# Pooled attention's denominators: from ones matmuls to running sums on ScalarE

## The chip, the cores and the metric

The kernel runs on one core of one Trainium2 chip. The metric is the device time of one execution in microseconds; the lower the better. Engines are named as in the profile: PE is TensorE, DVE VectorE, ACT ScalarE, POOL GpSimd, SP SyncE.

## The reference, cut to what matters

Four images of 256 channels and 32 x 32 pixels go through two residual blocks. The first is attention on the group-normalised image: half of it within windows of 2 x 2 pixels, half of it *pooled*, that is every pixel's query against 256 pooled windows. The second is a 3 x 3 convolution of the normalised, masked and rectified image.

```python
q = (xh.reshape(B, H * W, C) @ l_q_w).reshape(B, H * W, L_HEADS, HEAD_DIM)       # 4 heads of 32
pooled = xh.reshape(B, hg, WS, wg, WS, C).mean(axis=(2, 4)).reshape(B, G, C)     # G = 256
kv = (pooled @ l_kv_w).reshape(B, G, 2, L_HEADS, HEAD_DIM)
k, v = (kv[:, :, 0], kv[:, :, 1])
attn = jax.nn.softmax(jnp.einsum('bnhd,bmhd->bhnm', q, k) * SCALE, axis=-1)
lo = jnp.einsum('bhnm,bmhd->bnhd', attn, v).reshape(B, H * W, L_DIM)
lofi = (lo @ l_proj_w + l_proj_b).reshape(B, H, W, L_DIM)
...
x = x + _L0_conv_ref(_gn(x), ...)
x = x + _L1_conv_ref(_gn(x), ...)          # mask, relu, 3 x 3 convolution, bias
```

## The kernel before

Channels or tokens lie on the 128 partitions, and an image's 1024 pixels along the free dimension. Every engine has one program, written out by hand; semaphores tie them together, and each engine works in the order of its program. All four images go through the same steps. For TensorE an image has a *front* (projections of queries, keys and values; the scores of pooled attention; the scores of window attention) and a *rest* (exponentials' use: the value matmuls of both attentions and their output projections). The convolution of image b-1 is cut into single matmuls, and the program puts so many of them between the other steps as the tuples `FRONT` and `REST` (for image 1 `FRONT_1` and `REST_1`) say: `conv.more(fill[i])`. Half of the 144 matmuls of a convolution run in the rest of an image, the other half in the next front. In the front of image 2 another 8 (`POOL_WAIT`) go ahead of the pooled keys, in that of image 3 they go behind `fill[12]`. There are four PSUM tiles of two banks: `slot[0..2]` and `cps`, in which the convolution alternates between two banks. A new position of the convolution (`V_SUM`, `V_DIFF`, `V_LEFT`, `V_RIGHT`) begins only when VectorE has added the result of the position before the last to the image (`conv_result`).

Pooled attention needs the scores twice. In the front, TensorE makes eight blocks of *local scores* (L1113, tokens on partitions, 4 heads x 256 keys), which go round over three PSUM slots (`LA_SLOT`). VectorE takes the row maxima of each block (`maxima`, L848). A block may use its slot when the maximum three blocks ahead of it is done. The 32 columns of maxima are turned by TensorE (L1351), split into two parts (`maxima_parts`) and sent by SP's DMA into two more rows of the queries, so that the second scores (`pooled_scores`, keys on partitions) come out with the maximum already taken off. ScalarE exponentiates these into `probs` (`exp_scores`, L563). In the rest, `by_head` multiplies `probs` first by ones (the denominators, 16 matmuls in 32 records, ready signal `lden_pe`), then by the values (`lpv_pe`). VectorE turns the denominators in blocks, inverts them, turns them back (L1013 to L1016), multiplies (L1021) and gives the product to the output projection.

In the same front VectorE makes the sums and the mask of the convolution's input (`row_sums`, `column_sums`, `normalisation`, `mask_parts`, then `masked_image`, L784). The mask sum itself (`mask_sum`, L362) is made by GpSimd, whose program puts the four products of window attention (`products`, L379) ahead of it; these wait for the mask's parts (`mask_c`). ScalarE rectifies (`rectify`, L546), VectorE makes the convolution's positions (`conv_tiles`), ScalarE their high and VectorE their low parts (`conv_high`, L557; `conv_low`, L814, into `v_lo`). ScalarE also copies the window scores (`ssum_sb`, L591), which TensorE turns (L1361). Image 1 has an order of its own on VectorE (`second_front`).

## Time and profile before

| | |
|---|---|
| runs | 349.89, 351.33, 352.15 us; median 351.33 |
| profiled execution, first to last instruction | 347.5 us |
| busy: PE, PEld, DVE, ACT, POOL | 315.2, 222.3, 272.5, 148.8, 83.0 us |
| granted TensorE clock, mean | 0.979 of full speed |

The runs' times are of the whole execution on the device, the span counts from the first instruction to the last; the profiled execution has no time of its own beside its span, and 3.8 us lie between the span and the median of the runs. Starts and durations of the rows below are in microseconds from the span's start.

### The profile page before, as it was taken

The numbers are of one execution on the slowest core, as the hardware profiler recorded it, in microseconds if no ns is written. First come the engines' busy times: TensorE is split into PE (matmuls) and PEld (weight loads), VectorE is DVE, ScalarE is ACT, GpSimd is POOL, SyncE is SP. The second block draws the span as 40 slices with busy tenths as digits, with TensorE's granted clock in tenths as the row PEclk, the third lists the DMA queues.
The fourth block names the chain that finished last, engine by engine and source line by source line (L and its number), as shares of the span: only waits on it lengthen the run. The fifth ranks groups of instructions, "written<-read, shape, count | busy, mean of one in ns | idle before, by whom it ended". The sixth has DMA issues, their size and how long they took to land.

```text
span 347.5 us, 4162 instructions
## 1 busy us (share of the span) xinstructions
PE 315.2 (91%) x1566; PEld 222.3 (64%) x1566; DVE 272.5 (78%) x488; ACT 148.8 (43%) x189; POOL 83.0 (24%) x46
## 2 busy tenths in 40 slices
PE   0879968999979999999799999999799999999995
PEld 0566344267866663688567744888388727877884
DVE  4996668769999586889989767799887847897572
ACT  2442548464490843554047855351165423031300
POOL 2088513440436020003910200008600200202000
PEclk9999968899989999999999999999999999999999
DMA  8779500009700000099011200197001000101002
GB/s 276 276 102 140 228 5 0 2 1 134 94 0 4 2 1 2 0 130 159 1 63 41 82 1 2 35 128 128 4 0 62 0 0 5 58 0 62 0 0 121
DMA packets 12068, 20.38 MB, mean 59 GB/s; under 512 B 2065, under 2 KB 8081, under 8 KB 11793
## 3 DMA queue, kind: packets, MB, share of 16 engines
q1 hardware_dynamic: 12048, 20.13, 28.2%
q8 instruction: 12, 0.20, 0.2%
q14 instruction: 8, 0.06, 0.1%
HBM read 7.93 MB, written 4.19 MB: 35 GB/s over the span
## 4 chain that ended last, share of the span: by engine, by line
PE 58%; DVE 23%; ACT 8%; issue 6%; POOL 3%; DMA 2%; SPq 0%; DVEq 0%; POOLq 0%
PE slot L1113 29%; PE cps L1145 15%; PE slot L1189 7%; DVE l_max L848 3%; PE cps L1113 3%; DVE mask L784 3%; PE cps L1189 2%; ACT probs L563 2%; POOL probs L379 2%; DVE v_lo L814 1%; DMA xy<-x 1%; PE slot L1392 1%; ACT xn_hi L452 1%; ACT p_w L608 1%; DVE xn L740 1%
## 5 line engine op out<-in xcount | busy, mean ns | idle before, releaser
L1145 PE MATMUL cps<-v_hi,cw_hi 128*128 128x512 f32 (+1 forms) x144 | 57.6, 400 | 3.5 <-DVE v_lo L814 2.9
L1145 PE MATMUL cps<-v_hi,cw_lo 128*128 128x512 f32 (+1 forms) x144 | 57.9, 402 | 0.0
L1145 PE MATMUL cps<-v_lo,cw_hi 128*128 128x512 f32 (+1 forms) x144 | 56.4, 392 | 0.0
L379 POOL TENSOR_TENSOR probs<-q_w,k_w 128x1024 f32<-128x1024 f32 x14 | 32.9, 2376 | 79.5 <-DVE rw L777 72.3
L848 DVE TENSOR_REDUCE l_max<-slot 128x4 f32<-128x1024 f32 x32 | 37.1, 1216 | 5.9 <-PE slot L1113 5.9
L563 ACT ACTIVATE probs<-slot 128x1024 f32<-128x1024 f32 x32 | 31.4, 1021 | 16.0 <-PE slot L1113 15.9
L1145 PEld LDWEIGHTS cps<-v_hi,cw_hi 128*128 128x128 f32 x144 | 27.4, 191 | 12.7 <-issue 5.2
L1145 PEld LDWEIGHTS cps<-v_hi,cw_lo 128*128 128x128 f32 x144 | 27.4, 190 | 7.4 <-issue 2.2
L1145 PEld LDWEIGHTS cps<-v_lo,cw_hi 128*128 128x128 f32 x144 | 27.4, 190 | 5.0
L362 POOL TENSOR_TENSOR mask<-rw 128x1024 f32<-128x1024 f32 x8 | 15.2, 1912 | 56.6 <-DVE rw L777 56.6
L1113 PE MATMUL slot<-xn_hi,w_hi 128*128 128x512 f32 (+1 forms) x68 | 27.3, 401 | 1.1 <-ACT xn_hi L452 1.1
L1113 PE MATMUL slot<-xn_hi,w_lo 128*128 128x512 f32 (+1 forms) x68 | 26.1, 383 | 0.0
L1113 PE MATMUL slot<-xn_lo,w_hi 128*128 128x512 f32 (+1 forms) x68 | 25.9, 381 | 0.0
L546 ACT ACTIVATE xn<-mask 128x1024 f32<-128x1024 f32 x8 | 8.5, 1061 | 39.0 <-DVE mask L784 39.0
L557 ACT ACTIVATE v_hi<-mask 128x1024 fp32r<-128x1024 f32 x16 | 16.8, 1058 | 18.0 <-DVE mask L806 10.6
L1113 PE MATMUL slot<-probs,cst 128*32 128x512 f32 x176 | 23.1, 638 | 0.0
L1113 PE MATMUL slot<-qs,ks 98*128 98x512 f32 x64 | 21.4, 428 | 1.7 <-DMA qs<-probs 1.7
L1113 PEld LDWEIGHTS slot<-ks,qs 96*128 96x128 f32 x128 | 18.2, 194 | 6.3 <-DVE l_max L848 3.8
L814 DVE SCALAR_TENSOR_TENSOR v_lo<-mask,v_hi 128x1024 fp32r<-128x1024 f32 x16 | 19.2, 1220 | 3.6 <-ACT v_hi L557 3.6
L1113 PE MATMUL slot<-ks,qs 96*128 96x256 f32 x128 | 20.3, 293 | 1.2 <-DVE l_max L848 0.8
L427 POOL TENSOR_TENSOR q_w<-q_w,k_w 128x1024 f32<-128x1024 f32 x3 | 7.3, 2419 | 56.8 <-DVE k_w L986 56.8
L532 ACT ACTIVATE xn<-xy,gn 128x1024 f32<-128x1024 f32 x8 | 9.6, 1239 | 17.2 <-DVE gn L679 17.2
(197 smaller groups left out, 635.0 us busy)
## 6 DMA issues: line engine op xcount, KB each, us to landing
xy<-x SPq DMA_DIRECT2D x8, 512.0 KB, 6.6
out<-xy SPq DMA_DIRECT2D x8, 512.0 KB, 2.6
qs<-probs SPq DMA_DIRECT2D x12, 256.0 KB, 5.8
qs<-probs SPq DMA_DIRECT2D x24, 128.0 KB, 8.3
raw_cw<-conv_w SPq DMA_DIRECT2D x2, 1152.0 KB, 6.4
ks<-probs SPq DMA_DIRECT2D x12, 128.0 KB, 6.9
probs<-h_qkv SPq DMA_DIRECT2D x2, 192.0 KB, 3.8
probs<-l_kv SPq DMA_DIRECT2D x2, 128.0 KB, 3.7
```

What stands on the lines that cost most here:

```text
L362: nc.gpsimd.tensor_tensor(mask[:, k].rearrange("p (h w) -> p h w", h=H), rw[:, k, 0].unsqueeze(2).to_broadcast([P, H, W]), rw[:, k, 1].uns ...
L379: nc.gpsimd.tensor_tensor(product(b, j).rearrange("p (n w) -> p n w", n=NW), q_w[:].rearrange("p (n w) -> p n w", n=NW), k_w[:, j * G:(j + ...
L532: nc.scalar.activation(xn[:, k], img(b, k), ACT.Identity, bias=gn[1][:, 6, k:k + 1], scale=gn[1][:, 5, k:k + 1]).then_inc(yn_ready, 1)
L546: nc.scalar.activation(xn[:, k], mask[:, k], ACT.Relu).then_inc(relu, 1)
L557: nc.scalar.activation(v_hi[:, k, 2 * phase:2 * phase + 2].rearrange("p a b -> p (a b)"), mask[:, k], ACT.Copy, scale=TILE_SCALE[phase]).t ...
L563: nc.scalar.activation(probs[:, i], flat[score_slot(b, i)], ACT.Exp, scale=SCALE / NW)\
L784: nc.vector.scalar_tensor_tensor(mask[:, k], mask[:, k], -1.0, xn[:, k], ALU.max, ALU.mult).then_inc(masked, 1)
L814: nc.vector.scalar_tensor_tensor(v_lo[:, k, part].rearrange("p a b -> p (a b)"), mask[:, k], TILE_SCALE[phase], v_hi[:, k, part].rearrange ...
L848: nc.vector.tensor_reduce(l_max[:, bass.ds(n, HEADS, step=NB)], flat[LA_SLOT[n]].rearrange("p (h m) -> p h m", h=HEADS), AX_X, ALU.max, ne ...
L1113: return nc.tensor.matmul(dst, lhsT, rhs, start=start, stop=stop)
L1145: ins = nc.tensor.matmul(cps[:, pos % 2, y0 * WT:y1 * WT], (cw_hi, cw_hi, cw_lo)[part][:, k, pos, dy + 1, o * P:(o + 1) * P], (v_hi, v_lo, ...
L1189: ins = nc.tensor.matmul(last_bank(o, pos)[:, y0 * WT:y1 * WT], (cw_hi, cw_hi, cw_lo)[part][:, k, pos, dy + 1, o * P:(o + 1) * P], (v_hi, ...
```

## The change

The denominators are no longer made by ones matmuls in the rest. In the front, right behind VectorE's maximum of a block of local scores, ScalarE exponentiates the block in place in PSUM, one head at a time, with the negated maximum as bias and a running sum into `l_den` (`local_sums`, 32 instructions an image). So a block's slot is free when these sums are done (`la_den`) and no longer when the maximum is (`la_max`). VectorE inverts `l_den`, TensorE turns it, ScalarE copies the turned rows, SP writes them to DRAM and reads each head's row back to 32 partitions of `v_w`, once the window values are through with that tile (`spread_inverses`). The product waits for these transfers (`inv_in`) and for the value matmuls. Ones matmuls, block turns and their reciprocal go, and the residual of k = 0 comes behind the product.

The scale of the scores moves from the exponentials into the queries. The fill counts of `FRONT` are new. Loads come in another order: taps of k = 1, image 1, taps of k = 0, and only then the first stacking. ScalarE takes image 1's moments during image 0's projections and image 2's during image 1's attention, both of which it did in the fronts before. VectorE makes the masked image of k = 0 between the fifth and the sixth maximum, and no longer behind the eighth.

```diff
-FRONT = (0, 11, 0, 0, 4, 3, 3, 3, 3, 3, 6, 10, 18)
+FRONT = (0, 8, 0, 2, 5, 5, 5, 5, 5, 5, 6, 6, 12)
...
-        l_max = sb("l_max", [P, P])
+        l_max = sb("l_max", [P, NB * HEADS])
+        l_den = sb("l_den", [P, NB * HEADS])
+        l_inv = sb("l_inv", [NB * HEADS, P])
...
+        inv_rows = nc.dram_tensor("inv_rows", [B, NB * HEADS, P], F32).ap()
...
+            def spread_inverses(b):
+
+                sp.wait_ge(inv_sb, b + 1)
+                sp.dma_start(inv_rows[b], l_inv[:]).then_inc(inv_out, 16)
+                sp.wait_ge(inv_out, (b + 1) * 16)
+                sp.wait_ge(pv_ready, (b + 1) * NW)
+                for h in range(HEADS):
+                    row = inv_rows[b, h * NB:(h + 1) * NB].rearrange("n q -> (n q)").unsqueeze(0)
+                    sp.dma_start(v_w[HD * h:HD * (h + 1)], row.to_broadcast([HD, HW])).then_inc(inv_in, 16)
+
             def step(b, first, last):
 
+                spread_inverses(b)
                 if not last:
                     stack(b + 1)
...
-            for k in range(KT):
-                sp.dma_start(raw_cw[:, k].rearrange("p r d c -> p (r d c)"), cw[k]).then_inc(cw_in, 16)
+            taps_of(1)
+            load(1)
+            taps_of(0)
             stack(0)
-            load(1)
             load(2)
...
+            def local_sums(b, blocks):
+
+                for n in blocks:
+                    act.wait_ge(la_max, b * NB + n + 1)
+                    for h in range(HEADS):
+                        at = h * NB + n
+                        block = flat[LA_SLOT[n]][:, h * G:(h + 1) * G]
+                        last = nc.scalar.activation(block, block, ACT.Exp, bias=l_max[:, at:at + 1],
+                                                    accum_out=l_den[:, at:at + 1])
+                    last.then_inc(la_den, 1)
+
+            def inverses(b):
+
+                act.wait_ge(inv_pe, b + 1)
+                wait_count(act, inv_out, b * 16)
+                nc.scalar.copy(l_inv[:], slot[1][0:NB * HEADS, 1, 0:P]).then_inc(inv_sb, 1)
...
-                nc.scalar.copy(lq_hi, flat[0]).then_inc(lq_act, 1)
+                nc.scalar.activation(lq_hi, flat[0], ACT.Copy, scale=SCALE / NW).then_inc(lq_act, 1)
...
-                if b == 1:
+                if first:
+                    local_sums(b, range(NB - 1))
+                elif b == 1:
+                    local_sums(b, range(3))
                     for k in range(KT):
                         rectify(0, k)
                     conv_high(0, 0)
                     act.wait_ge(lv_pe, 1)
                     values_of(cps)
-                if not last and not late:
-                    for done in stacked_late:
-                        act.wait_ge(done, (b + 1) * STACK_LATE)
-                    input_moments(b + 1, 0)
-                if b > 1:
+                    local_sums(b, range(3, NB))
+                else:
+                    local_sums(b, range(6))
                     rectify(b - 1, 0)
+                    local_sums(b, range(6, NB))
                 act.wait_ge(ssum_pe, b + 1)
                 nc.scalar.copy(q_w[:], flat_cps if first else flat[0]).then_inc(ssum_sb, 1)
+                if first:
+                    local_sums(b, range(NB - 1, NB))
+                inverses(b)
                 if b > 1:
                     rectify(b - 1, 1)
...
+            def local_inverses(b):
+
+                dve.wait_ge(la_den, (b + 1) * NB)
+                nc.vector.reciprocal(l_den[:], l_den[:]).then_inc(den_c, 1)
...
-                maxima(b, range(6))
+                maxima(b, range(5))
+                if not first:
+                    masked_image(b - 1, 0)
+                maxima(b, range(5, 6))
                 older_result(V_SUM)
                 maxima(b, range(6, NB))
                 maxima_parts(b)
                 older_result(V_DIFF)
                 if not first:
-                    for k in range(KT):
-                        masked_image(b - 1, k)
-                    conv_tiles(b - 1, 0, 0)
+                    masked_image(b - 1, 1)
+                local_inverses(b)
+                if not first:
+                    conv_tiles(b - 1, 0, 0)
                 window_maxima(b)()
...
-                for i in range(2):
-                    h = slice(i * HALF, (i + 1) * HALF)
-                    dve.wait_ge(lden_pe, b * 2 + i + 1)
-                    ins = nc.vector.transpose(v_w[:, h], flat[2][:, h])
-                link(ins)
-                link(nc.vector.reciprocal(inv, blocks[:, :, 0]))
-                link(nc.vector.transpose(blocks, inv.unsqueeze(2).to_broadcast([P, HW // HD, HD])))
-                if not last:
-                    residual(b, 0, 1)
-                dve.wait_ge(blocks_c, (b + 1) * N_BLOCKS)
+                dve.wait_ge(inv_in, (b + 1) * SPREAD)
                 dve.wait_ge(lpv_pe, b + 1)
                 nc.vector.tensor_tensor(side_by_side(q_w), by_window(flat[0]), by_window(v_w[:]),
                                         ALU.mult).then_inc(lnorm, 1)
+                if not last:
+                    residual(b, 0, 1)
...
                     else:
-                        pe.wait_ge(la_max, b * NB + n - 2)
+                        pe.wait_ge(la_den, b * NB + n - 2)
...
                 pe.wait_ge(la_max, (b + 1) * NB)
-                nc.tensor.transpose(slot[2][:, 0, 0:P], l_max[:], cst[:, C_ID:C_ID + P]).then_inc(lmt_pe, 1)
+                pe.wait_ge(la_den, b * NB + 6)
+                nc.tensor.transpose(slot[2][0:NB * HEADS, 0, 0:P], l_max[:], cst[:, C_ID:C_ID + P]).then_inc(lmt_pe, 1)
                 conv.more(fill[10])
                 if not first:
+                    pe.wait_ge(la_den, b * NB + 7)
                     window_scores(b, slot[0])
...
+                pe.wait_ge(den_c, b + 1)
+                nc.tensor.transpose(slot[1][0:NB * HEADS, 1, 0:P], l_den[:], cst[:, C_ID:C_ID + P]).then_inc(inv_pe, 1)
                 pe.wait_ge(max_stacked, (b + 1) * MAX_STACK)
-                for i in range(2):
-                    pooled_scores(b, i)
+                pooled_scores(b, 0)
+                pe.wait_ge(inv_sb, b + 1)
+                pooled_scores(b, 1)
...
-                by_head(2, lambda t, h: cst[:, C_ONE:C_ONE + HD], lden_pe)
+                values_by_head()
                 if not last:
                     window_out()
-                by_head(0, lambda t, h: lv[:, t, HD * h:HD * (h + 1)], lpv_pe)
```

## Rows read from the trace of the kernel before

**Rows 1.** The page, the chain that ended last: its shares of the span by engine.
```profile
PE 58%; DVE 23%; ACT 8%; issue 6%; POOL 3%; DMA 2%; SPq 0%; DVEq 0%; POOLq 0%
```

**Rows 2.** Timeline of the rest of image 1, TensorE: start, length, then line, names, shapes, count.
```profile
130.55 3.64 PE L1113 MATMUL slot<-probs,cst 128*32 128x512 f32 x32
...
134.12 1.98 PE L1113 MATMUL slot<-k_w,w_out 128*128 128x512 f32 x4
...
136.04 3.64 PE L1113 MATMUL slot<-probs,lv 128*32 128x512 f32 x32
```

**Rows 3.** Timeline of the front of image 2, VectorE and GpSimd.
```profile
161.60 6.87 DVE L848 TENSOR_REDUCE l_max<-slot 128x4 f32<-128x1024 f32 x6
...
161.86 9.41 POOL L379 TENSOR_TENSOR probs<-q_w,k_w 128x1024 f32<-128x1024 f32 x4 [34.52 <-DVE rw L777]
171.23 3.78 POOL L362 TENSOR_TENSOR mask<-rw 128x1024 f32<-128x1024 f32 x2
```

**Rows 4.** Timeline of the front of image 2, TensorE; idle before and releaser in brackets.
```profile
169.19 0.50 PE L1145 MATMUL cps<-v_hi,cw_hi 128*128 128x512 f32 x1 [0.40 <-DVE xy L889]
...
171.45 0.33 PE L1351 MATMUL slot<-cst,l_max 128*128 128x128 f32 x1 [1.54 <-DVE l_max L848]
...
185.06 0.47 PE L1145 MATMUL cps<-v_hi,cw_hi 128*128 128x512 f32 x1 [0.80 <-DVE v_lo L814]
```

**Rows 5.** Timeline of the rest of image 0, TensorE.
```profile
59.30 5.34 PE L1113 MATMUL slot<-probs,cst 128*32 128x512 f32 x32
```

**Rows 6.** Timeline of the front of image 2, ScalarE.
```profile
150.19 0.39 ACT L500 ACTIVATE lv<-slot 128x256 f32<-128x256 f32 x1
150.46 1.06 ACT L466 ACTIVATE probs<-xy 128x1024 bf16<-128x1024 f32 x1
151.41 0.20 ACT L466 ACTIVATION_READ_ACCUMULATOR probs<-xy 128x1 f32 x1
151.50 1.05 ACT L467 ACTIVATE probs<-xy 128x1024 bf16<-128x1024 f32 x1
```

**Rows 7.** Groups of instructions by line and shape: busy us, mean ns | idle before, releaser.
```profile
L532 ACT ACTIVATE xn<-xy,gn 128x1024 f32<-128x1024 f32 x8 | 9.6, 1239 | 17.2 <-DVE gn L679 17.2
L546 ACT ACTIVATE xn<-mask 128x1024 f32<-128x1024 f32 x8 | 8.5, 1061 | 39.0 <-DVE mask L784 39.0
```

**Rows 8.** Timeline of the front of image 0, VectorE and TensorE.
```profile
30.80 6.92 DVE L848 TENSOR_REDUCE l_max<-slot 128x4 f32<-128x1024 f32 x6 [3.03 <-PE slot L1113]
...
33.21 0.74 PE L1113 MATMUL slot<-ks,qs 96*128 96x256 f32 x4 [0.39 <-DVE l_max L848]
```

**Rows 9.** Timeline of the front of image 1, ScalarE and TensorE.
```profile
94.77 2.20 ACT L546 ACTIVATE xn<-mask 128x1024 f32<-128x1024 f32 x2 [2.99 <-DVE mask L784]
...
99.66 0.47 PE L1145 MATMUL cps<-v_hi,cw_hi 128*128 128x512 f32 x1 [2.08 <-DVE v_lo L814]
...
113.13 2.01 ACT L557 ACTIVATE v_hi<-mask 128x1024 fp32r<-128x1024 f32 x2
...
113.59 1.04 PE L1361 MATMUL slot<-cst,q_w 128*128 128x128 f32 x8
```

**Rows 10.** One line's instructions, 173 to 178 us: ns least, median, most; first and last start.
```profile
L784 DVE SCALAR_TENSOR_TENSOR mask<-mask,xn x2: 1212/2066/2920, 173.2 to 176.0; 128x1024 f32<-128x1024 f32 x2
```

**Rows 11.** Timeline of the front of image 3, VectorE and TensorE.
```profile
235.85 6.87 DVE L848 TENSOR_REDUCE l_max<-slot 128x4 f32<-128x1024 f32 x6
...
245.70 0.33 PE L1351 MATMUL slot<-cst,l_max 128*128 128x128 f32 x1 [2.27 <-DVE l_max L848]
...
260.14 0.39 PE L1145 MATMUL cps<-v_hi,cw_hi 128*128 128x512 f32 x1
260.37 0.39 PE L1145 MATMUL cps<-v_lo,cw_hi 128*128 128x512 f32 x1
```

**Rows 12.** DMA issues by line: size of each, median us from issue to landing.
```profile
qs<-probs SPq DMA_DIRECT2D x24, 128.0 KB, 8.3
```

**Rows 13.** One stretch of 1 us: busy us of each engine, granted clock, DMA share, GB/s.
```profile
102.00:103.00 1.00, 1.00 (x5) 0.92 (x4) 1.00 (x2) 1.00 (x3) 1.00 (x1) 0.50 0.00 0
```

More of the change, by code:

```diff
@@ L40 @@
 LIN = 2.0 / (H - 1)
-C_ID, C_GRP, C_HEAD, C_ONE = 0, P, 2 * P, 2 * P + HD
-C_IX = C_ONE + HD
+C_ID, C_GRP, C_HEAD = 0, P, 2 * P
+C_IX = C_HEAD + HD
 C_IXR = C_IX + H
@@ L84 @@
 WARM = (4, 1)
[L87 removed]
+N_FIRST, N_GN, N_MASK, N_SOFT, N_POOL, N_FOLD = 4, 12, 15, 7, 4, 4
 SOFT_READ = 2
@@ L188, in build @@
         x_in = [[sem(f"x_in{b}_{k}") for k in range(KT)] for b in range(B)]
-        cw_in, c_in, cst_in = sem("cw_in"), sem("c_in"), sem("cst_in")
+        c_in, cst_in = sem("c_in"), sem("cst_in")
+        cw_in = [sem(f"cw_in{k}") for k in range(KT)]
         w_in = [sem(f"w_in{i}") for i in range(len(PIECES))]
@@ L223, in build @@
         st_pe, st_exp = sem("st_pe"), sem("st_exp")
-        lden_pe, blocks_c, fold_c = sem("lden_pe"), sem("blocks_c"), sem("fold_c")
+        la_den, den_c, inv_pe = sem("la_den"), sem("den_c"), sem("inv_pe")
+        inv_sb, inv_out, inv_in = sem("inv_sb"), sem("inv_out"), sem("inv_in")
+        fold_c = sem("fold_c")
         lpv_pe, lnorm = sem("lpv_pe"), sem("lnorm")
@@ L528, in projections @@
                     nc.scalar.copy(dst[:], src).then_inc(qkv_sb, 1)
+                    if first and i == 0:
+                        weight_high(0, V_RIGHT, 2)
+                    if first and i == 1:
+                        input_moments_of(1, 1, v_w[:])
+                        act.wait_ge(moments[0], 2 * KT)
             def normalise_y_of(b, k):
@@ L573, in step @@
                     nc.scalar.copy(sel[:].rearrange("p a b -> p (a b)"), raw_sel).then_inc(sel_act, 1)
-                late = b + 1 == RING
                 projections(b, first)
@@ L599, in step @@
                     conv_high(b - 1, 0)
-                if not last and not late:
-                    act.wait_ge(moments[0], (b + 2) * KT)
                 exp_scores(b, range(2))
@@ L610, in step @@
                     exp_scores(b, range(2, LT - NW))
-                if late:
+                if not first and not last:
                     input_moments(b + 1, LT - NW)
@@ L961, in front @@
                 if not first:
-                    for k in range(KT):
-                        masked_image(b - 1, k)
+                    masked_image(b - 1, 1)
+                local_inverses(b)
+                if not first:
                     conv_tiles(b - 1, 0, 0)
@@ L1237, in pooled_scores, with values_by_head @@
                 last.then_inc(st_pe, 1)
-            def by_head(s, lhsT, ready):
+            def values_by_head():
                 for half in range(2):
@@ L1243, in by_head @@
                         for h in range(HEADS):
-                            last = mm(slot[s][HD * h:HD * (h + 1), half], lhsT(t, h), probs[:, h * MT + t, halves(half)],
-                                      t == 0, t == MT - 1)
-                    if ready is lden_pe or half == 1:
-                        last.then_inc(ready, 1)
+                            last = mm(slot[0][HD * h:HD * (h + 1), half], lv[:, t, HD * h:HD * (h + 1)],
+                                      probs[:, h * MT + t, halves(half)], t == 0, t == MT - 1)
+                last.then_inc(lpv_pe, 1)
             def window_scores_of(b, j, to):
```

38 lines of the change are left out of this document (17 added, 21 removed).

## The prediction

> **What bounds the kernel now.** I read the chain of work that ended last first: 58% of the span lies on TensorE and 23% on VectorE [rows 1]. So a matmul that goes is worth its length only in a stretch where TensorE is what ends last, and a new wait costs what TensorE then stands. Second, the timeline of TensorE where an image's pooled attention ends. The ones matmuls of image 1 stand from 130.55 to 134.12, then the window output, then the value matmuls from 136.04, without a gap [rows 2]: there every microsecond of TensorE is on the path. Third, the timelines of the stretch before it, the front of the next image, where the change puts its new work. In the fronts of images 2 and 3 the three small engines hand work to each other: VectorE starts the eight row maxima at 161.60, GpSimd starts its four products at 161.86 and its two mask sums at 171.23 [rows 3]; TensorE waits for the last maximum until 171.45 and for VectorE's `v_lo` until 185.06 [rows 4]. In what follows T is the start of the first maximum of a front (161.60 in image 2, 235.85 in image 3).
>
> **What goes.** The ones matmuls: 134.12 - 130.55 = 3.57 us in each of images 1 to 3 [rows 2]. In image 0 they took 5.3 us [rows 5], but because the clock was at its lower level; the value matmuls would come to stand in that slow stretch, so what goes there is again the second set's 3.6. The block turns, the reciprocal between them and the residual that moves behind the product were under the value matmuls; after the change VectorE's product needs only the values and the inverses. What is late next is ScalarE's split of the next image, which waits for the same value matmuls; it follows them. I take 3.6 + 3.5 + 3.5 + 3.6 = **14.2 us saved**.
>
> **What a local sum costs.** The trace has no exponential of 256 columns with a per-partition bias and a running sum, so I build it. Two plain 256-column passes follow each other in 0.27 us (150.19, 150.46). A pass with a running sum is followed by a read of the accumulator, and the next pass starts 0.09 us after that read starts (151.41, 151.50) [rows 6]. Two per-partition operands make a 1024-column pass 1239 instead of 1061 ns, 0.09 each [rows 7]. So 0.27 + 0.09 + 0.10 = 0.46 us a head and 4 x 0.46 = **1.84 us a block**, 14.7 an image. The bounds are 4 x 0.27 = 1.1 (read and bias hidden) and 4 x 0.65 = 2.6 (the read, 0.19 us long, not overlapped at all). I take 1.84, the sum of nearest rows. Writing to PSUM in place shows in no row; none says it is dearer. The Trainium skill ("ScalarE: Activation LUTs", What ACT_TABLE_LOAD costs) gives an ACTIVATE with a pointer bias about 280 + 0.833 N ns, of which about 93 overlap with the next; by that page's figures, an estimate, 0.40 us a head and 1.6 a block. It has no price for the accumulator read, which the trace shows; with 1.6 the sum below would be about 1.3 us lower.
>
> **Front of image 0.** The fourth score block now waits for the first sum, the fifth for the second. The first maximum starts at 30.80 and takes 1.2; the second sum ends at 32.1 + 2 x 1.84 = 35.8, where the fifth block started at 33.21 [rows 8]. From there TensorE's order (a score block, then a window product) is longer than 1.84, so the delay does not grow; the turn of the denominators and the copy of the inverses add a little. Cost **+2.85**.
>
> **Front of image 1.** ScalarE does three sums, 5.5 us, before it rectifies the masked image; it stood idle 2.99 there [rows 9], so the rectified image, and with it the start of the convolution (99.66, which already waits for `v_lo`), is 2.5 late. Then ScalarE copies the inverses before it makes the second half of the convolution's input: it must await TensorE's turns (113.59, 0.9 us long), the turn of the denominators (0.3) and copy them (0.3), so 115.1 instead of 113.13. Cost 2.5 + 1.95 = **+4.4**.
>
> **Front of image 2.** Here lies the largest term. VectorE's new order is five maxima, the masked image of k = 0, the sixth maximum, a convolution result, the last two maxima. The masked image needs GpSimd's mask sum, and that stands behind four products which start only when the mask's parts are done, that is at T: 9.4 + 1.9 us later [rows 3], T + 11.6. No line of the change moves this. The fifth maximum ends at about T + 6.9 (its scores wait for the second sum, T + 1.3 + 3.7, and take half a microsecond; a maximum takes 1.15 [rows 3]). So VectorE stands 4.7 us, and behind it in its queue stand three maxima that used to be over at T + 9.8. The masked image then runs beside GpSimd's second mask sum; the trace has it at 2.92 us there and 1.21 alone [rows 10]; I take 2.92, the same neighbour, and keep 1.7 less for each of the two images as the bound. T + 14.5. Sixth maximum 15.7, result 16.3. TensorE needs that result to go on with the convolution: a wait for it shows at 169.19 [rows 4]; it is the start of the third position of the second output half, 36 convolution matmuls after this front begins to fill. With the new counts 8 + 8 + 0 + 2 + 5 + 5 + 5 = 33 stand ahead of the sixth score block, so the point comes three matmuls behind it, at T + 8. So TensorE stands from T + 8 to T + 16.4, and only then issues the seventh and eighth score blocks. Last maximum T + 20.3, its turn at T + 20.4; it was at 171.45, T + 9.85. From that turn to the restart of the convolution there were 185.06 - 171.45 = 13.6 us. The fills in it have 24 matmuls where they had 34, 10 x 0.23 = 2.3 less (260.14 to 260.37 [rows 11]); the reciprocal, the turn and the copy of the inverses put in 1.1. So T + 32.8 instead of T + 23.5: **+9.4**.
>
> **Front of image 3.** The same, but this front begins to fill without the first 8 matmuls, so the convolution's point comes behind the eighth score block, and only the maxima wait: last maximum T + 18.6, turn T + 18.7. It was 245.70, and the next convolution started at 260.14, 14.4 later [rows 11]; now 14.4 - 2.3 + 1.1 = 13.2, so T + 31.9 instead of T + 24.3: **+7.6**.
>
> **At nothing**, with the cover named: the scaled copy of the queries and its rest (same shapes); the turn of 32 rows instead of 128; image 2's moments, moved into the attention of image 1, where ScalarE's exponentials wait for TensorE; image 1's moments and the loads' new order (the loads are done long before they are read, and the split weights now end just when the first maximum begins; bound +0.6). SP now waits, ahead of the next image's stacking and the stores, for the inverses and then for the window values; what is queued behind it is not due before the next front, and stores are only due at the end. The spread must land before the value matmuls end, about 7 us after its last wait. The nearest row, 128 KB transfers in a row of six, has 8.3 us to landing [rows 12]; four of them have less queue. TensorE's fill hides a part more. I take 0; the far end is a rival.
>
> **Sum**: -14.2 + 2.85 + 4.4 + 9.4 + 7.6 = +10.05 us on a span of 347.5, 357.5. The median of the runs lies 3.8 above the span (351.3), so **361 us**, 2.8% more. A half-speed clock could add to it: after TensorE had stood before 99.66 for 2.08 us the granted clock was 0.50, the 1.2 GHz level, around 102 to 103 [rows 9, 13], and the new stalls are longer. At that level 12 matmuls of fill take some 2.5 us more, but VectorE's maxima set the pace behind each stall; I add nothing and keep 0 to 2.5 for both together. The Trainium skill ("TensorE: Matmul & The Clock Gate", Part 1) makes the lower level the state after idleness; by that rule both stalls would be followed by it, and the sum would come to an estimated 361 + 2.5 = 363.5.
>
> **Rivals.** (a) *Faster*: the fronts of images 2 and 3 absorb the sums. Place: VectorE's masked image; it decides by whether GpSimd's mask sum is there when the fifth maximum ends. If so, and with sums at 1.1 us, image 0's fifth block waits until 32.1 + 2.2 = 34.3 (+1.3 with the small steps), image 1 pays 3 x 1.1 - 2.99 + 1.95 = 2.3, and ScalarE's eight sums end at T + 10, ahead of the window scores, 0.5 and 0 in images 2 and 3; 351.3 - 14.2 + 4.1 = **341**. For it: convolution matmuls stand ready as filling, and TensorE has most of the path. Against it: the products' time [rows 3], by which the mask sum is 4.7 us too late. (b) *Same*: no wait for the mask sum, but sums at 1.84: they and the rectifying end at T + 1.3 + 14.7 + 1.0 = 17.0, the window scores' copy at 18.1, and the steps from that copy to the convolution, 8.1 by the rows of image 2 (177.1 to 185.06), end at T + 26.2 instead of 23.5 and 24.3. The fronts cost 2.85 + 4.4 + 2.7 + 1.9 = 11.85, **349**. (c) Sums at 2.6: ScalarE sets the pace of all eight blocks, and images 0 and 1 lose some 10 more: **374**. (d) The spread lands 3 us after the values in each image; TensorE's fill hides 1.1 of it, 4 x 1.9 on the forecast: **368**.
>
> **How the numbers follow.** Forecast 0.65 (355 to 366, from the bounds of the masked image, the sums and the clock), (a) 0.13, (b) 0.09, (c) 0.05, (d) 0.08. One per cent, 3.5 us, is about what a measurement of this kernel tells from none. Slower by more: 0.63 + 0.05 + 0.08 = 0.76; within: 0.02 + 0.09 = 0.11; faster: 0.13. The range 347 to 369 leaves out (a) and (c), 0.18.
>
> **What would show it.** In the profile after: accumulating exponentials 0.46 us apart; VectorE idle some 5 us before the masked image of k = 0 in images 2 and 3, released by GpSimd; TensorE standing near 8 us behind the sixth score block of image 2; the last maximum at T + 20 and T + 18.6; window output 3.6 us earlier after the last exponential; no wait of VectorE's product on a DMA. I am wrong if GpSimd's mask sum is not what VectorE waits for, or if TensorE's stalls in the fronts were in truth time that a later wait would have taken anyway.

## The result, and the profile after

The changed kernel took 366.72 us in the median of four runs (365.78 to 368.57), the kernel before 351.08 (349.89 to 352.15; a fourth execution beside the three above): 1.050 times as long, 95% interval 1.045 to 1.056, or 15.6 us. The profiled execution took 366.0 us with a span of 363.9, where the one before had 347.5: 16.4 more. Executions of one and the same kernel differ by some 5 us, the longer ones at a lower mean granted clock: of the twelve of inverses_late, a kernel of the experiments below, five lie at 345.5 to 345.8 us with 0.974 to 0.975 of full speed, and four at 350.1 to 350.3 with 0.950 to 0.955.

The page after, the span, the row of busy time, the clock row and the costliest groups that are new or changed (line, engine, operation, count | busy us, mean ns | idle before, releaser):

```profile
span 363.9 us, 4192 instructions
...
PE 310.3 (85%) x1442; PEld 223.7 (61%) x1442; DVE 259.4 (71%) x476; ACT 208.5 (57%) x449; POOL 82.0 (23%) x45
...
PEclk9999885899989999999679899999879999999999
...
L1193 PE MATMUL cps<-v_hi,cw_hi 128*128 128x512 f32 (+1 forms) x144 | 60.5, 420 | 21.7 <-DVE xy L942 13.0
L506 ACT ACTIVATE slot<-slot,l_max 128x256 f32<-128x256 f32 x128 | 57.9, 482 | 18.3 <-DVE l_max L896 18.3
...
v_w<-inv_rows SPq DMA_DIRECT2D x16, 128.0 KB, 2.7
```

TensorE works less and waits more: 4.9 us of its work are gone (315.2 before), ScalarE has 60 more, and the convolution stands 13.0 us in three places for VectorE's convolution results (7.97 us in image 2, 4.81 in image 3). The transfers of the inverses land in 2.7 us; no wait of VectorE's product names them.

TensorE's waits after (who, for whom: us in all, times, the longest):

```profile
PE cps L1193 <- DVE xy L942: 13.0, 3, 8.0
...
PE slot L1161 <- ACT slot L506: 7.2, 6, 2.4
PE cps L1193 <- DVE v_lo L861: 6.4, 2, 4.0
```

Before, the first of these stood at 0.6 us in all, the third at 2.9, and the second was not there.

To see where the time went I cut both spans at the same instructions of TensorE (starts from its timelines: first score block, group means, first projection, pooled output) and laid the prediction's terms beside:

| stretch | before | after | difference | forecast |
|---|---|---|---|---|
| image 0: first score block to the next image's group means | 29.06 | 35.59 | +6.53 | +2.85 |
| from there to image 1's first projection | 13.95 | 10.14 | -3.81 | -3.6 |
| image 1: first projection to group means | 57.28 | 61.17 | +3.89 | +4.4 |
| from there to the pooled output | 11.07 | 7.32 | -3.75 | -3.5 |
| image 2: image 1's pooled output to group means | 61.87 | 74.77 | +12.90 | +9.4 |
| from there to the pooled output | 11.32 | 7.54 | -3.78 | -3.5 |
| image 3: image 2's pooled output to window output | 63.35 | 70.99 | +7.64 | +7.6 |
| from there to the pooled output | 11.09 | 7.86 | -3.23 | -3.6 |
| ahead of all that, and behind it | 88.51 | 88.52 | 0.0 | 0 |
| span | 347.50 | 363.90 | +16.40 | +10.05 |

The savings came as forecast, and so did images 1 and 3. Images 0 and 2 lost 3.7 and 3.5 us more.

The timeline of the front of image 2 after, VectorE and GpSimd [rows 3] (start, length, engine, line; idle before and releaser in brackets; T is 164.42):

```profile
164.42 3.48 DVE L896 TENSOR_REDUCE l_max<-slot 128x4 f32<-128x1024 f32 x3
...
170.26 1.23 DVE L896 TENSOR_REDUCE l_max<-slot 128x4 f32<-128x1024 f32 x1 [0.60 <-PE slot L1161]
175.96 2.91 DVE L831 SCALAR_TENSOR_TENSOR mask<-mask,xn 128x1024 f32<-128x1024 f32 x1 [4.47 <-POOL mask L383]
178.80 1.21 DVE L896 TENSOR_REDUCE l_max<-slot 128x4 f32<-128x1024 f32 x1
179.93 0.73 DVE L942 SCALAR_TENSOR_TENSOR xy<-cps,cbias,xy 128x512 f32<-128x512 f32 x1
...
185.77 1.23 DVE L896 TENSOR_REDUCE l_max<-slot 128x4 f32<-128x1024 f32 x1 [1.71 <-PE slot L1161]
...
164.68 9.38 POOL L400 TENSOR_TENSOR probs<-q_w,k_w 128x1024 f32<-128x1024 f32 x4 [30.92 <-DVE rw L824]
174.02 3.77 POOL L383 TENSOR_TENSOR mask<-rw 128x1024 f32<-128x1024 f32 x2
```

And TensorE in the same stretch [rows 4], with the granted clock of two windows (length, busy time of PE, PEld, DVE, ACT, POOL, then the clock):

```profile
180.72 0.80 PE L1193 MATMUL cps<-v_hi,cw_hi 128*128 128x512 f32 x1 [7.97 <-DVE xy L942]
181.74 1.05 PE L1161 MATMUL slot<-ks,qs 96*128 96x256 f32 x4
184.68 1.05 PE L1161 MATMUL slot<-ks,qs 96*128 96x256 f32 x4
187.05 0.28 PE L1397 MATMUL slot<-cst,l_max 128*32 128x128 f32 x1 [0.16 <-DVE l_max L896]
...
199.42 0.76 PE L1193 MATMUL cps<-v_hi,cw_hi 128*128 128x512 f32 x1 [2.48 <-DVE v_lo L861]
...
203.75 0.63 PE L1161 MATMUL slot<-qs,ks 98*128 98x512 f32 x2
```

```profile
175.00:185.00 10.00, 4.28 (x13) 3.66 (x14) 5.93 (x4) 3.78 (x13) 2.79 (x2) 0.52 0.00 0
200.00:205.00 5.00, 5.00 (x18) 4.09 (x17) 5.00 (x12) 3.21 (x4) 0.00 (x0) 0.72 0.09 36
```

VectorE stands 4.47 us until GpSimd's mask sum is there; behind it wait three maxima and a result, and for the result TensorE stands 7.97 us. The mask sum is there at T + 11.5 (forecast 11.6), TensorE goes on at T + 16.3 (16.4). From there the rows part from the forecast: TensorE runs at its 1.2 GHz level (granted clock 0.52 of full speed from 175 to 185 us), the last maximum ends at T + 22.6 and not T + 20.3, the convolution restarts at T + 35.0 and not T + 32.8.

### The profile page after: what moved, and what is told of

It is laid out like the page before. It is cut to its first block, busy times and chain, and to the rows that moved or that the text cites. A ratio compares the mean times of both kernels' runs of the same rounds, so it can differ in the third digit from the quotient of the medians.

```text
span 363.9 us, 4192 instructions
## 1 busy us (share of the span) xinstructions
PE 310.3 (85%) x1442; PEld 223.7 (61%) x1442; DVE 259.4 (71%) x476; ACT 208.5 (57%) x449; POOL 82.0 (23%) x45
## 4 chain that ended last, share of the span: by engine, by line
PE 53%; DVE 22%; ACT 11%; issue 6%; POOL 5%; DMA 1%; SPq 0%; DVEq 0%; POOLq 0%; ACTq 0%
PE slot L1161 24%; PE cps L1193 15%; PE slot L1237 7%; POOL probs L400 4%; PE cps L1161 4%; ACT slot L506 4%; PE cps L1237 2%; DVE l_max L896 2%; ACT probs L609 2%; DVE v_lo L861 2%; DVE mask L831 2%; DMA xy<-x 1%; PE slot L1442 1%; POOL mask L383 1%; DVE xy L942 1%
## 5 line engine op out<-in xcount | busy, mean ns | idle before, releaser
L1193 PE MATMUL cps<-v_hi,cw_hi 128*128 128x512 f32 (+1 forms) x144 | 60.5, 420 | 21.7 <-DVE xy L942 13.0
L506 ACT ACTIVATE slot<-slot,l_max 128x256 f32<-128x256 f32 x128 | 57.9, 482 | 18.3 <-DVE l_max L896 18.3
L1193 PE MATMUL cps<-v_hi,cw_lo 128*128 128x512 f32 (+1 forms) x144 | 59.3, 412 | 0.0
L1193 PE MATMUL cps<-v_lo,cw_hi 128*128 128x512 f32 (+1 forms) x144 | 58.4, 405 | 0.0
L896 DVE TENSOR_REDUCE l_max<-slot 128x4 f32<-128x1024 f32 x32 | 38.1, 1220 | 16.1 <-PE slot L1161 16.1
L1193 PEld LDWEIGHTS cps<-v_hi,cw_hi 128*128 128x128 f32 x144 | 28.6, 199 | 31.8 <-DVE xy L942 14.2
L1193 PEld LDWEIGHTS cps<-v_lo,cw_hi 128*128 128x128 f32 x144 | 28.8, 200 | 6.0 <-issue 1.1
L1193 PEld LDWEIGHTS cps<-v_hi,cw_lo 128*128 128x128 f32 x144 | 28.5, 198 | 6.2 <-issue 0.7
L506 ACT ACTIVATION_READ_ACCUMULATOR slot<-slot,l_max 128x1 f32 x128 | 30.9, 241 | 0.0
L1161 PE MATMUL slot<-ks,qs 96*128 96x256 f32 x128 | 22.7, 310 | 7.6 <-ACT slot L506 7.2
L831 DVE SCALAR_TENSOR_TENSOR mask<-mask,xn 128x1024 f32<-128x1024 f32 x8 | 13.6, 1714 | 11.0 <-POOL mask L383 11.0
```

The costliest lines, as they stand in the source:

```text
L506: last = nc.scalar.activation(block, block, ACT.Exp, bias=l_max[:, at:at + 1], accum_out=l_den[:, at:at + 1])
L831: nc.vector.scalar_tensor_tensor(mask[:, k], mask[:, k], -1.0, xn[:, k], ALU.max, ALU.mult).then_inc(masked, 1)
L896: nc.vector.tensor_reduce(l_max[:, bass.ds(n, HEADS, step=NB)], flat[LA_SLOT[n]].rearrange("p (h m) -> p h m", h=HEADS), AX_X, ALU.max, ne ...
L1161: return nc.tensor.matmul(dst, lhsT, rhs, start=start, stop=stop)
L1193: ins = nc.tensor.matmul(cps[:, pos % 2, y0 * WT:y1 * WT], (cw_hi, cw_hi, cw_lo)[part][:, k, pos, dy + 1, o * P:(o + 1) * P], (v_hi, v_lo, ...
```

## The experiments

Theory W is the prediction's: fronts 2 and 3 lose by VectorE standing for the mask sum. Theory S says that the sums on ScalarE make the chain, and another wait would take the time anyway. K says that TensorE's lower clock behind a gap costs as much as the gap. All kernels' ratios are to the kernel before, beside runs of it on the same chip (medians 349.7 to 350.7 us).

**late_masks**, the order undone:

```diff
-                maxima(b, range(5))
-                if not first:
-                    masked_image(b - 1, 0)
-                maxima(b, range(5, 6))
+                maxima(b, range(6))
                 older_result(V_SUM)
...
                 older_result(V_DIFF)
-                    masked_image(b - 1, 1)
+                    for k in range(KT):
+                        masked_image(b - 1, k)
...
-                    local_sums(b, range(6))
+                    local_sums(b, range(NB))
                     rectify(b - 1, 0)
-                    local_sums(b, range(6, NB))
```

> The changed kernel with VectorE's and ScalarE's old order in the fronts of images 2 and 3: both masked images behind the second convolution result, the rectifying behind all eight local sums. Theory W (the front's loss is VectorE standing for GpSimd's mask sum): the stands of 4.5 and 4 us or so before the masked image go, the maxima follow each other at the pace of the sums (1.8 us a block), the convolution restarts near T + 26 instead of T + 35.0 and T + 32; 8 to 10 us come back in image 2 and 5 to 6 in image 3, so 366.7 - 15 = 352, between 348 and 355. Theory S (the sums on ScalarE are the chain, and a later wait takes the stand's time): at least 362.

Measured 350.43 us, ratio 1.0015 (0.997 to 1.006): all of the loss against the kernel before is gone. Its timelines of image 2, VectorE's first and last maximum, then TensorE going on behind the convolution result, its eighth score block and the restart (lines from L895 on stand for L896 and so on, since it is a line shorter):

```profile
168.42 3.48 DVE L895 TENSOR_REDUCE l_max<-slot 128x4 f32<-128x1024 f32 x3
...
180.88 1.23 DVE L895 TENSOR_REDUCE l_max<-slot 128x4 f32<-128x1024 f32 x1 [0.39 <-PE slot L1158]
...
178.02 0.50 PE L1190 MATMUL cps<-v_hi,cw_hi 128*128 128x512 f32 x1 [1.28 <-DVE xy L941]
...
180.20 0.64 PE L1158 MATMUL slot<-ks,qs 96*128 96x256 f32 x4
...
194.54 0.47 PE L1190 MATMUL cps<-v_hi,cw_hi 128*128 128x512 f32 x1 [2.52 <-DVE v_lo L860]
```

The restart is at T + 26.1. All sums are still made, so S is out as the explanation of the loss; what S says is true of what is left: 26.1 instead of 23.5 before.

**mask_sum_first**, the wait taken away at its other end:

```diff
+                if b > 1:
+                    mask_sum(b - 1, b + 1)
                 products(b)
...
-                    if b > 1:
-                        mask_sum(b - 1, b + 1)
```

> The changed kernel with one thing moved: in images 2 and 3 GpSimd makes its two mask sums (3.8 us) before the four products (9.4 us), not after. VectorE's and ScalarE's order stays as the change made it. Theory W: the mask sum is there at T + 1.9, VectorE makes the masked image with no stand, and TensorE's wait for the convolution result falls from 8.0 to about 3 us in image 2; products end at T + 13.2, which is before the window scores are due (the sums end near T + 17). 351 us, between 347 and 355. Theory S: no gain, 362 or more. Third, P: the products are what comes late then, and 3.8 us an image go back: 358 to 360.

Measured 356.55 us, ratio 1.019 (1.014 to 1.024): 10 us back, and 1.6 above the range that I gave. The rows of image 2, VectorE, GpSimd, TensorE (T is 166.55):

```profile
173.53 2.91 DVE L831 SCALAR_TENSOR_TENSOR mask<-mask,xn 128x1024 f32<-128x1024 f32 x1
...
166.89 3.78 POOL L383 TENSOR_TENSOR mask<-rw 128x1024 f32<-128x1024 f32 x2 [31.04 <-DVE rw L824]
170.63 10.36 POOL L400 TENSOR_TENSOR probs<-q_w,k_w 128x1024 f32<-128x1024 f32 x4
...
178.29 0.79 PE L1193 MATMUL cps<-v_hi,cw_hi 128*128 128x512 f32 x1 [3.42 <-DVE xy L942]
...
196.25 0.47 PE L1193 MATMUL cps<-v_hi,cw_hi 128*128 128x512 f32 x1 [2.49 <-DVE v_lo L861]
```

VectorE's stand is gone (no bracket), TensorE's wait is 3.4 us as expected. But the masked image still takes 2.91 us between the maxima, now beside the products, and TensorE is still left at the lower clock behind its gap (1.00 from 173 to 178 us, 0.66 from 178 to 183); the restart is at T + 29.7. Theory P does not hold: the last maximum, at T + 17.3, comes behind the products' end.

**before_early_mask**, the same order in the kernel before, with no sums at all:

```diff
-                maxima(b, range(6))
+                maxima(b, range(5))
+                if not first:
+                    masked_image(b - 1, 0)
+                maxima(b, range(5, 6))
                 older_result(V_SUM)
...
-                    for k in range(KT):
-                        masked_image(b - 1, k)
+                    masked_image(b - 1, 1)
```

> The kernel before with nothing of the change but VectorE's order in the fronts of images 2 and 3: five maxima, the masked image of k = 0, the sixth maximum, the convolution result, two maxima. No local sums on ScalarE, the ones matmuls stay. Theory W: the last maximum comes at T + 18.6 instead of T + 9.85, and most of that 8.75 is on the path in both images: 351 + 2 x 8 = 367, between 361 and 371. Theory S: with no sums on ScalarE the order alone costs little, 351 to 355.

Measured 370.13 us, ratio 1.059 (1.053 to 1.066). Its rows of image 2:

```profile
163.30 5.74 DVE L848 TENSOR_REDUCE l_max<-slot 128x4 f32<-128x1024 f32 x5
174.83 2.91 DVE L784 SCALAR_TENSOR_TENSOR mask<-mask,xn 128x1024 f32<-128x1024 f32 x1 [5.79 <-POOL mask L362]
...
179.60 0.79 PE L1147 MATMUL cps<-v_hi,cw_hi 128*128 128x512 f32 x1 [9.14 <-DVE xy L889]
...
196.93 0.47 PE L1147 MATMUL cps<-v_hi,cw_hi 128*128 128x512 f32 x1 [0.82 <-DVE v_lo L814]
```

The order alone makes the old kernel 20 us slower, without one local sum. With late_masks this shows W from both sides.

**no_denominators**, what there is to save. Ones matmuls, block turns and their reciprocal are left out of the kernel before:

```diff
-                by_head(2, lambda t, h: cst[:, C_ONE:C_ONE + HD], lden_pe)
...
-                    ins = nc.vector.transpose(v_w[:, h], flat[2][:, h])
...
-                link(nc.vector.reciprocal(inv, blocks[:, :, 0]))
-                link(nc.vector.transpose(blocks, inv.unsqueeze(2).to_broadcast([P, HW // HD, HD])))
```

> The kernel before without the ones matmuls, the block turns and the reciprocal between them, in all four images; VectorE's product takes the window values in place of the inverses, and the residual stands behind it. It leaves the denominators of the pooled attention out. This measures what the change can save at most: by my sum 14.2, so 337 us, between 335 and 339. If the block turns, the reciprocal and the turned order hid behind the value matmuls less than I took, more is saved (333); if VectorE's product or ScalarE's split is late next, less (342).

Measured 342.82 us, ratio 0.981 (0.976 to 0.986): 7 us, half of my sum. TensorE's waits gave the reason; this one was not in the kernel before:

```profile
PE slot L1102 <- DVE gn L693: 3.1, 3, 2.5
```

I had left the window output ahead of the value matmuls, and it waits for VectorE's first step of the next image's normalisation, which the ones matmuls had covered.

**no_denominators_2**, with the change's order:

```diff
-                if not last:
-                    window_out()
                 by_head(0, lambda t, h: lv[:, t, HD * h:HD * (h + 1)], lpv_pe)
+                if not last:
+                    window_out()
```

> As no_denominators (the kernel before without ones matmuls, block turns and reciprocal; the denominators of the pooled attention are left out), but with the value matmuls ahead of the window output in images 0 to 2, as the change has them. In no_denominators the window output stood first and TensorE waited 3.1 us in three images for the next image's group statistics, in image 0 for 2.46 us with the lower clock behind it. If that wait ate the missing saving, this gives my 14.2 back: 337 (334 to 340). If the saving is not there in any order, 342 again.

Measured 337.07 us, ratio 0.965 (0.961 to 0.970), 13.6 us below the 350.7 beside it. The saving of 14.2 is there, and 6 us of it hang on the order of two groups of matmuls that the change turned round.

**one_head_sums**, what the sums themselves cost, on late_masks: one head's sums are made, 1.0 stands for the other three denominators.

```diff
-                    for h in range(HEADS):
+                    for h in range(1):
                         at = h * NB + n
...
+            nc.gpsimd.memset(l_den[:, NB:], 1.0).then_inc(zeroed, 1)
```

> late_masks with the local sums of one head in four: 8 passes of 256 columns an image instead of 32, and 1.0 in place of the other three heads' denominators (they are left out). All else, the spread of the inverses too, stays. If the sums' pace on ScalarE is what still eats the saving (image 0's score blocks and the clock behind them 5 us, the rectified image of image 1 2.5, 2 to 3 in each of images 2 and 3), this is 350 - 12 = 338, between 335 and 342. If the spread, the inverses' copy or the turn eats it, at least 346.

Its four executions took 337.28, 344.71, 344.94 and 345.40 us, at mean granted clocks of 0.990, 0.963, 0.955 and 0.955. The first is what the forecast says, the others lie between the forecast and the rival's 346, so the times alone decide nothing. The trace of the first does, cut at the same instructions. In image 0 it goes back to the steps of the kernel before: 13.8 us from the first score block to the turn of the maxima (13.3 before, 17.4 after). From the first score block to the end of the span it needs 305.4 us, late_masks 318.7 (its trace is of an execution of 353.79 us, 3.4 above its median), and no_denominators_2, which has neither sums nor spread, 301.8. So 13.3 of the 16.9 us between those two go with the passes of three heads and with the clock behind them: most of what late_masks still loses is the sums' pace. The fourth head's passes, the spread, the copy and the turn are not free: they cost 3.6 us together, 1.9 of them in image 1, where ScalarE copies the inverses ahead of the convolution's input.

**products_in_gap_0**, for K, on late_masks:

```diff
+                    if first and NB - NW - 1 <= n < NB - 1:
+                        pe.wait_ge(qkv_sb, 3)
+                        window_scores_of(b, n - NB + NW + 1, cps)
+                    if n > 2:
+                        pe.wait_ge(la_den, b * NB + n - 2)
                     for h in range(HEADS):
...
-                    if first and n >= NB - NW:
-                        pe.wait_ge(qkv_sb, 3)
-                        window_scores_of(b, n - NB + NW, cps)
```

> late_masks with image 0's window products one block earlier on TensorE: they stand ahead of the fourth to seventh score blocks, in the time in which TensorE stood waiting for ScalarE's sums (2.4 us before the fourth block), not behind the fifth to eighth. Theory K (image 0 lost to a gap in TensorE and to the 1.2 GHz level behind it): the gap is filled, the granted clock stays at 1.00 there, and the turn of the maxima comes some 13.5 us after the first score block instead of 17.4 to 18.1; 3 to 4 us come back, 346.5. Rival: the sums set the pace of that stretch anyway, at most 1 us: 349.5 to 350.5.

Measured 348.93 us, ratio 0.997 (0.994 to 1.001). In the changed kernel's image 0, TensorE [rows 8]:

```profile
33.78 0.74 PE L1161 MATMUL slot<-ks,qs 96*128 96x256 f32 x4 [2.40 <-ACT slot L506]
35.60 1.22 PE L1161 MATMUL slot<-ks,qs 96*128 96x256 f32 x4 [1.09 <-ACT slot L506]
36.75 2.97 PE L1161 MATMUL cps<-mask,cst 128*32 128x512 f32 x4
...
47.15 0.28 PE L1397 MATMUL slot<-cst,l_max 128*32 128x128 f32 x1
```

and in this kernel:

```profile
31.26 1.90 PE L1158 MATMUL cps<-mask,cst 128*32 128x512 f32 x4
33.66 0.74 PE L1158 MATMUL slot<-ks,qs 96*128 96x256 f32 x4 [0.50 <-ACT slot L506]
...
44.36 0.28 PE L1394 MATMUL slot<-cst,l_max 128*32 128x128 f32 x1 [1.98 <-DVE l_max L895]
```

The gap ahead of the fourth block is filled. From the first score block to the turn of the maxima the granted clock is 1.00 (0.90 in the changed kernel, 0.81 in late_masks), the pair of window products takes 1.90 instead of 2.97 us, and the turn comes 14.7 us after the first score block instead of 17.4 (18.1 in late_masks); it comes at 14.7 in the three later kernels with this edit as well. So much of K is shown: the lower level behind this gap goes with the gap. That it costs as much as the gap is not shown. To image 1's first projection the trace needs 40.5 us instead of late_masks's 45.5, but two later kernels with the same instructions in image 0, tiles_in_wait and early_start_1, need 43.4 and 42.7. The median gives back only 1.5 us, which lies between K's 346.5 and the rival's 349.5, and the intervals of the two ratios overlap. The gap was not the only place that brings the lower level: this trace still has it in image 0 behind the turn, at 0.53 from 46 to 49 us and at 0.50 from 60 to 63.

**inverses_late**, on late_masks:

```diff
-                inverses(b)
                 if b > 1:
                     rectify(b - 1, 1)
                 if b == 1:
                     conv_high(0, 1)
+                inverses(b)
```

> late_masks with ScalarE's copy of the inverses behind the second half of the convolution's input in image 1 (and behind the second rectifying in images 2 and 3). By my term for it (1.95 us in image 1) 348.5. Rival: TensorE's second pooled score waits for that copy and loses as much: 350.4 or more.

Measured 347.18 us, ratio 0.995 (0.991 to 0.9995), 3.2 below late_masks. Image 1 from its first projection to its pooled output takes 66.7 us instead of 69.5 (69.5 and 69.6 in mask_sum_first and products_in_gap_0, which have the old place of the copy too). The rival is out.

**three_moves**, **tiles_in_wait** and **early_start_1** build on each other; the edits of the last two:

```diff
-                window_maxima(b)()
+                rest_of_softmax = window_maxima(b)
+                if not first:
+                    conv_tiles(b - 1, 1, 0)
+                rest_of_softmax()
...
-FRONT_1 = (0, 0, 0, 0, 0, 0, 0, 9, 5, 9, 7, 6, 0)
+FRONT_1 = (0, 0, 0, 0, 0, 0, 9, 3, 4, 7, 7, 6, 0)
...
-                    local_sums(b, range(3))
+                    local_sums(b, range(2))
...
-                    local_sums(b, range(3, NB))
+                    local_sums(b, range(2, NB))
...
-                    elif starting and n == 5:
+                    elif starting and n == 4:
                         weights_ready()
```

> late_masks, products_in_gap_0 and inverses_late together. If the three losses lie in different images and add, 350.4 - 1.5 - 3.2 = 345.7, between 343 and 348, and faster than the kernel before by 1.4%. If one hides the other (the clock behind one gap falls in the next), 347 to 349, no measurable difference.

> three_moves, and in the fronts of images 2 and 3 VectorE makes the convolution's tiles of k = 1 while it waits for the exponential of the window scores (1.0 us idle there, 1.3 us of tiles), not behind it. The restart of the convolution comes 1.0 us earlier in both images if VectorE is what ends last there (it waits for v_lo): 2 us less than three_moves, 344. If not, the same as three_moves.

> tiles_in_wait, and in image 1 ScalarE makes two local sums ahead of the rectifying and the first half of the convolution's input, not three, and TensorE begins the convolution behind the fifth score block, not the sixth. By my term for image 1 (2.5 us for the rectified image behind three sums, 1.8 of them the third) the convolution starts some 2 us earlier and 2 us come back: 342. If the maxima behind it set the pace (VectorE has five left), 344 as before.

Measured: three_moves 346.92 us, ratio 0.992 (0.988 to 0.996); tiles_in_wait 343.98, 0.985 (0.980 to 0.989); early_start_1 343.53, 0.985 (0.980 to 0.989). The last two are faster than both kernels, by 6 us (1.5%) than the one before and by 23 than the changed one. three_moves gives 1.2 us less than the sum of its parts would. The restart in tiles_in_wait is only 0.4 us earlier, T + 25.1 for 25.5, and images 2 and 3 are 0.4 us shorter each; so the rows give 0.8 of the 2.9 us between those two medians to its edit, and nothing here shows where the rest comes from. In early_start_1 image 1 from its first projection to its pooled output takes 64.9 us for 66.9 and 67.2 in the two others: the 2 us are there, but neither the medians nor the spans (341.8 and 342.0) show them. The profiled execution of early_start_1 came to its first score block 3.1 us later than that of tiles_in_wait, ahead of all edits: its granted clock was 0.52 from 20 to 27 us, that of tiles_in_wait 1.00.

## Why the prediction was right, and where its sizes were off

The 366.72 us lie in the range, but 0.7 above the 355 to 366 that the forecast gave itself, and nearer to rival (d)'s 368 than to the forecast's 361. That it was the forecast's mechanism, and not (d), stands in the rows and not in the time. By the spans the sum is short by 6.35 us: images 0 and 2 by 3.7 and 3.5, less 0.5 in image 1 and 0.4 in the savings. The 3.8 us that the sum adds from span to median hid 1.0 of it; after, they are 2.8.

**The savings** were sized right: 14.6 us in the two traces, 13.6 in no_denominators_2, for 14.2.

**A local sum**: the passes stand 0.45 us apart (0.46 forecast), 1.8 us a block. The Trainium skill's figures ("ScalarE: Activation LUTs", What ACT_TABLE_LOAD costs) gave an estimate of 0.40 without the read of the accumulator; the rows say 0.45 with it.

**The mask sum's wait**, the largest term, has the right mechanism: VectorE's 4.47 us in image 2 and 4.49 in image 3, TensorE's 8.0, the step in its place at T + 16.3. Image 3 is right throughout: last maximum at T + 18.5 (18.6), restart at T + 31.5 (31.9). In image 1 both parts are right: the convolution starts 2.0 us later (2.5), the second half of its input another 1.8 (1.95).

**The mis-sized term is the clock.** I wrote "I add nothing and keep 0 to 2.5 for both together". In image 2 the stretch from TensorE's restart to the eighth score block took 3.96 us (180.72 to 184.68); in late_masks, at a granted clock of 1.00, the same instructions took 2.18 (178.02 to 180.20). That is 1.8 us on the path, since TensorE and not VectorE's maxima set the pace there: VectorE stood 1.71 us for the last block. Then the restart at 199.42, after a gap of 2.48 us, ran at the lower level as well (0.50 from 199.4 to 202.4): 4.33 us to the next pooled score at 203.75, 1.5 more than the 2.80 before, from 185.06 [rows 4] to this row:

```profile
187.86 0.63 PE L1113 MATMUL slot<-qs,ks 98*128 98x512 f32 x2
```

Together 3.3 of the 3.5 us by which image 2 missed. The second part is not a fixed price of such a gap. At the same place the granted clock fell behind 2.53 us in products_in_gap_0 too (0.52 from 186 to 189), but stayed at 1.00 behind 2.52 us in late_masks (194.5 to 199.5), 2.49 in mask_sum_first (196.2 to 201.2) and 2.52 in one_head_sums (179.4 to 184.4).

**Image 0** I gave 2.85 us and no clock at all. TensorE stood 2.40 us ahead of the fourth block and 1.09 ahead of the fifth, and what followed ran at half speed: 1.07 us in one pair of window products. Up to the turn of the maxima it lost 4.1 us; another 2.4 behind it, up to the group means, where the granted clock was 0.50 from 56 to 61 us. TensorE's same matmuls in that part, before and after:

```profile
53.09 0.70 PE L1113 MATMUL slot<-qs,ks 98*128 98x512 f32 x2
...
56.31 1.36 PE L1113 MATMUL slot<-qs,ks 98*128 98x512 f32 x4
```

```profile
57.40 1.05 PE L1161 MATMUL slot<-qs,ks 98*128 98x512 f32 x2
...
62.52 1.24 PE L1161 MATMUL slot<-qs,ks 98*128 98x512 f32 x4
```

From the first to the second row 3.22 us became 5.12: 1.9 of the 2.4 is clock. The turn of the denominators, for which TensorE waits 1.22 us, delays nothing there: the first pooled score follows the turn of the maxima after 3.8 us, and after 4.0 before, when it waited for the maxima's DMA. The kernel before had a stretch at the lower level in this part too (0.52 from 46.5 to 53.5 us), and the place of it moves from run to run (below), so the 1.9 is the price in this execution. The Trainium skill's rule ("TensorE: Matmul & The Clock Gate", Part 1), that the lower level follows idleness, would have put image 0 on the list as well as images 2 and 3, and I used it for two. The trace agrees with it in all three: 0.57 from 35 to 39 us, 0.52 from 175 to 185, 0.50 from 261 to 267.

**The small terms at nothing** held: the spread lands in 2.7 us, and the moments, the loads and SP's queue show in no new wait of TensorE.

The rivals: (a) and (b) needed the mask sum in time, and it was not; late_masks is rival (b) made real, at 350.4 for its 349, with the restart at T + 26.1 for its 26.2. (c) is out by the 0.45 us of a pass, (d) by the 2.7 us to landing. The 374 of (c) did not follow from its terms, which make 361 + 10 = 371; nothing rests on it.

## What to carry to other kernels

A step that is moved up in an engine's queue waits for its inputs with all that stands behind it: before moving it, look up when each input is ready, on the engine that makes it. What a change saves can be real to the microsecond and still be lost in an order that it brings along; so undo the order and the work one at a time, each in the kernel that has only the other. And where a change opens a gap on TensorE, allow for what may follow the gap at the lower clock, above all where TensorE sets the pace behind it; here it followed the stands of 8.0 and 4.8 us, and two of five gaps of 2.5 us at one and the same place.

## What the runs showed of the hardware that was not expected

**A slow pair.** VectorE's masked image takes 1.20 us alone and 2.91 beside GpSimd's mask sum, which the rows before showed [rows 10]. New is that its neighbour need not be the mask sum: beside the products in mask_sum_first (173.53) it takes 2.91 as well. The rows fit two engines that take turns: there the second product would end at 170.63 + 2 x 2.35 = 175.33, the masked image ends 1.1 us later (176.44), its own length, and the four products take 1.0 us more than alone (10.36 for 9.38). So the masked image, put beside GpSimd's, costs the remainder of GpSimd's instruction as well. Not every step of VectorE pays: the row maxima, which read PSUM, run beside the same products at 1.23 us (170.26 in the changed kernel's image 2), as they do alone, and the four products keep their 9.38.

**Running sums keep their pace while their records grow.** ScalarE's timeline after, the first and the 20th pass of an unbroken row of 20 in image 3:

```profile
248.90 0.45 ACT L506 ACTIVATE slot<-slot,l_max 128x256 f32<-128x256 f32 x1 [0.97 <-DVE l_max L896]
249.27 0.19 ACT L506 ACTIVATION_READ_ACCUMULATOR slot<-slot,l_max 128x1 f32 x1
249.37 0.44 ACT L506 ACTIVATE slot<-slot,l_max 128x256 f32<-128x256 f32 x1
...
257.46 0.55 ACT L506 ACTIVATE slot<-slot,l_max 128x256 f32<-128x256 f32 x1
257.81 0.31 ACT L506 ACTIVATION_READ_ACCUMULATOR slot<-slot,l_max 128x1 f32 x1
```

A pass's record grows from 0.45 to 0.55 us and the read's from 0.19 to 0.31, but 19 passes lie in 8.56 us, 0.45 each. The mean of the group, 482 ns, is not the price; the distance of the starts is.

**The lower clock moves.** three_moves and tiles_in_wait have the same instructions in image 0. From the turn of the maxima to the group means the one took 15.5 us and the other 18.6. In the first the granted clock was 0.68 from 46 to 51 us, then 0.98 and 1.00; in the second it stayed at 0.50 for ten. Windows of the first and of the second:

```profile
51.00:56.00 5.00, 3.28 (x17) 2.29 (x17) 4.52 (x9) 3.88 (x4) 0.28 (x1) 0.98 0.02 5
```

```profile
49.00:54.00 5.00, 4.27 (x14) 2.72 (x12) 4.32 (x8) 3.03 (x5) 0.00 (x0) 0.50 0.02 5
54.00:59.00 5.00, 4.75 (x12) 3.73 (x12) 2.47 (x3) 3.08 (x4) 3.62 (x2) 0.50 0.00 0
```

On a single core of this kernel a difference below 1% therefore shows in a cut of the traces at the same instructions rather than in a handful of medians, and a cut needs the clock of its stretch beside it.
